# Moments in pairs on GpSimd, a seventh tile on VectorE, and a later adjacency load in the first stage of a graph kernel

## The chip, the cores and the metric

The kernel runs on one core of one Trainium2 chip. The metric is the device time of one execution in microseconds (us). The core has five engines with their own instruction streams: TensorE (PE, and PEld for its weight loads), VectorE (DVE), ScalarE (ACT), GpSimd (POOL) and SyncE (SP), which here only issues DMAs. They wait for each other by semaphores.

## The reference

```
def _layernorm(x):  m = mean(x); v = var(x); return (x - m) / sqrt(v + 1e-5)

h  = relu(_layernorm(x))                  # x: 8192 x 128
Wh = h @ W;  src = Wh @ a[:128];  dst = Wh @ a[128:]
e  = leaky_relu(src + dst.T, 0.2)         # 8192 x 8192
att = softmax(where(adj > 0, e, -9e15), axis=1)
h_prime = att @ Wh
...                                       # GRU cell with w_ih, w_hh, b_ih, b_hh on (h_prime, h)
x  = x + gru(h_prime, h)
h  = relu(_layernorm(x))
x  = x + adj @ (h @ W1.T + b1)
```

adj is an 8192 x 8192 float32 matrix of zeros and ones (256 MB).

## The kernel before, in words

The kernel has three stages. All run on five engines at once, each with its own loop. The order of work is written out by hand, and each instruction that another one needs raises a semaphore.

**First stage.** x lies in SBUF as 64 tiles H[:, t, :] of 128 rows x 128 columns. Eight DMAs bring eight tiles each (L264). VectorE makes the moments of a group q of eight tiles in `stats(q)`: bn_stats for each tile (L642), which leaves the mean and the sum of squared differences of the even and of the odd elements apart, bn_aggr, which joins them to mean and variance (L646), and the addition of EPS (L649). GpSimd raises the result to the power -0.5 in `deviation(q)` (L395). Then `normalised(q)` on VectorE: the product of mean and 1/deviation (L656), and `BY_DVE` = 6 of the eight tiles normalised (L659). ScalarE does the two others (L465). VectorE's order is stats(q+1), then normalised(q). TensorE transposes four tiles at a time (L999, k = 0 to 15, two for each q) into PSUM, ScalarE copies them with Relu (`column(k)`, L451), TensorE multiplies them with W and the two columns W @ a (`weighted(k)`, L987), and ScalarE copies the result to WG (`features(k)`, L455). TensorE may start the transposes only once VectorE has copied W @ a to wext (L672), which stands behind normalised(0).

SP's queue is in order too: for each k it waits for column(k) and stores it to memory (L275), for each odd k it stores eight tiles of H as rows (L278), and behind k = 7 and k = 15 it issues the loads of the first two pieces of the adjacency, X[0] and X[1], 2 MB each (L281). column(k) also waits until the store of column(k-4) has landed, whose buffer it reuses.

Then the tables. VectorE's instructions in order, the first of them right behind normalised(7):

```
ones_of(0, 0, 0, 0)                       # L692: X[0] -> bytes, waits for the load of X[0]
dve.wait_ge(p_ev, 16)                     # the last features()
... L699 to L714: largest and least of dst, signs, thresholds
table_product(0): L720 x2 (times TSCALE), then L728
```

ScalarE makes two tables of exponentials in between (L479, L480) and, behind them, calls one Sigmoid so that its table of functions is loaded (L483). table_product and table_low (VectorE, L728 and L733) and table_high (ScalarE, L490) make the tables TB for 16 groups; in row block 0 this is interleaved with the masks.

**Second stage.** 32 row blocks of 256 rows, four pieces c of each. VectorE makes ones of the adjacency (L692) and part of the sign masks (L743), ScalarE the others (L506), VectorE joins them (L751, L755), and TensorE multiplies masks and tables (L1014), 64 matmuls for each of 256 products. The GRU of earlier row blocks runs in between; its weights GW are made on GpSimd once (L416 to L420), right behind deviation(7) once their loads have landed, and its biases too (L401 to L412). **Third stage.** adj times the second features (L1104).

Of the kernel before, what the change touches and what calls it, by code (L numbers as in the profile page):

```python
# [1 line left out]

# [4 lines left out]
F = 128  # L7
P = 128
# [10 lines left out]
SLOPE = 0.2  # L19
# [5 lines left out]
EPS = 1e-5  # L25
# [7 lines left out]
TSCALE = 2048.0  # L33
# [9 lines left out]
GROUP = 5  # L43
COUNTED = (NS - 1) * CS
LATE = CS + 25
BY_DVE = 6

f32 = mybir.dt.float32
f16 = mybir.dt.float16
# [4 lines left out]
ALU = mybir.AluOpType  # L54
# [23 lines left out]
def binary_adjacency(nc, sem, q_out, redo, xb, adjb, w, wt, a, wiht, whht, b_ih, b_hh, w1t, b1, out):  # L78
    ctx = ExitStack()
    with ctx:  # L80
# [12 lines left out]
        JK = sb("JK", [P, 8 * TW])  # L93
# [55 lines left out]
        sdx = JK[:, 530:530 + NT]  # L149
        rsx = JK[:, 600:600 + NT]  # L150
        nmx = JK[:, 670:670 + NT]
        BG = X1[0].bitcast(bf16)
        bt, dt_ = BB[:, 0:NT], BB[:, NT:2 * NT]
        wtt = X1[0][:, 0:F]
# [49 lines left out]
        t_sc = k_w = sem("t_sc")  # L204
        d_hi = t_lo
        d_hh, d_hl = sem("d_hh"), sem("d_hl")
        g_sum = p_wa
        g_bb = p_ab
        g_pre = sem("g_pre")
# [50 lines left out]
        with nc.Block() as block:  # L260
            @block.sync
            def _(sp):
# [10 lines left out]
                for k in range(16):  # L273
                    sp.wait_ge(p_ht, k + 1)
                    sp.dma_start(ht_d[:, k * 512:(k + 1) * 512], hTq[k % 4]).then_inc(p_htout[k % 4], 16)  # L275
                    if k % 2:
                        q = k // 2
                        sp.dma_start(h_d[:, q * 8:(q + 1) * 8, :], H[:, q * 8:(q + 1) * 8, :]).then_inc(p_hout, 16)  # L278
                    if k in (7, 15):
                        b = k // 15  # L280
                        sp.dma_start(X[b][:, :], adjb[b, :, :]).then_inc(c_in[b], 16)  # L281
                    if k == 9:
                        sp.wait_ge(p_bias, 8)
                        for part in range(3):
                            sp.dma_start(b_d[part, :, :], bpart[part]).then_inc(b_in, 16)
# [90 lines left out]
            @block.gpsimd  # L376
            def _(pool):
                nc.gpsimd.memset(ident[:, :], 0.0).then_inc(p_id, 1)
                nc.gpsimd.memset(ones[:, :], 1.0)
                nc.gpsimd.memset(epst, EPS)  # L380
                nc.gpsimd.memset(half, -0.5)
                nc.gpsimd.memset(onesb[:, :], 1.0)
                nc.gpsimd.memset(nz[:, LATE - CS - 16:16, 2 * CS + 1:2 * CS + 2], 0.0)
                nc.gpsimd.memset(BI[:, :], 0.0).then_inc(p_one, 1)
                nc.gpsimd.memset(bhid, 0.0).then_inc(p_bias, 1)
                pool.wait_ge(p_id, 1)
                nc.gpsimd.affine_select(out=ident[:, :], in_=ident[:, :], compare_op=ALU.not_equal, fill=1.0,
                                        base=0, pattern=[[-1, P]], channel_multiplier=1).then_inc(p_id, 1)
                nc.gpsimd.memset(WG[:, :, F + 2:F + 3], 1.0).then_inc(p_one, 1)
                pool.wait_ge(p_one, 1)  # L390

                def deviation(q):
                    pool.wait_ge(p_sd, q + 1)
                    at = slice(q * 8, q * 8 + 8)
                    nc.gpsimd.tensor_tensor(rsx[:, at], sdx[:, at], half[:, 0:1].to_broadcast([P, 8]), ALU.pow).then_inc(  # L395
                        p_rs, 1)

                for q in range(4):
                    deviation(q)
                pool.wait_ge(p_wa, 1)  # L400
                nc.gpsimd.memset(X1[0], 0.0)  # L401
                pool.wait_ge(b_in, 80)
                nc.gpsimd.tensor_tensor(brow, brow, bhid, ALU.add).then_inc(p_bias, 1)
                pool.wait_ge(p_bias, 2)
                nc.gpsimd.tensor_scalar(brow[0:4, :], brow[0:4, :], WSCALE, None, ALU.mult).then_inc(p_bias, 1)
                src = [brow] + bres
                for k in range(3):
                    pool.wait_ge(p_bias, 2 * k + 3)
                    nc.gpsimd.tensor_copy(bpart[k], src[k]).then_inc(p_bias, 1)
                    if k < 2:  # L410
                        pool.wait_ge(p_bias, 2 * k + 4)
                        nc.gpsimd.tensor_tensor(bres[k], src[k], bpart[k], ALU.subtract).then_inc(p_bias, 1)  # L412
                for q in range(4, 8):
                    deviation(q)
                pool.wait_ge(wt_in, 64)
                nc.gpsimd.tensor_scalar(wraw, wraw, WSCALE, None, ALU.mult).then_inc(p_bias, 1)  # L416
                pool.wait_ge(p_bias, 9)
                nc.gpsimd.tensor_copy(GW[:, 0, :, :], wrawv).then_inc(p_bias, 1)
                pool.wait_ge(p_bias, 10)
                nc.gpsimd.tensor_tensor(GW[:, 1, :, :], wrawv, GW[:, 0, :, :], ALU.subtract).then_inc(p_bias, 1)  # L420
                pool.wait_ge(p_id, 2)
                nc.gpsimd.tensor_copy(identh[:, :], ident[:, :]).then_inc(p_bias, 1)

                def slot(g, u, k):
                    if in_range(g, 2):
                        q = g - 2
                        pool.wait_ge(d_mv, q + 1)
                        nc.gpsimd.tensor_tensor(ve, mv[:, :, 1:2].rearrange("p t k -> p (t k)"),  # L428
                                                epst[:, 0:1].to_broadcast([P, 2]), ALU.add).then_inc(d_ve, 1)
                        pool.wait_ge(d_ve, q + 1)  # L430
                        nc.gpsimd.tensor_tensor(rstd, ve, half, ALU.pow).then_inc(g_rs, 1)  # L431

                each_row_block(pool, slot)
                for g in range(NS, NS + 2):
                    slot(g, g % 2, g // 2)
# [200 lines left out]

            @block.vector
            def _(dve):
                def stats(q):
                    dve.wait_ge(p_x[q], 16)  # L640
                    for t in range(q * 8, q * 8 + 8):
                        ins = nc.vector.bn_stats(stx[:, t, :], H[:, t, :])  # L642
                    ins.then_inc(p_st, 1)
                    dve.wait_ge(p_st, q + 1)
                    for t in range(q * 8, q * 8 + 8):
                        ins = nc.vector.bn_aggr(mvx[:, t, :], stx[:, t, :])  # L646
                    ins.then_inc(p_mv, 1)
                    dve.wait_ge(p_mv, q + 1)
                    nc.vector.tensor_scalar(sdx[:, q * 8:(q + 1) * 8],  # L649
                                            mvx[:, q * 8:(q + 1) * 8, 1:2].rearrange("p t k -> p (t k)"), EPS, None,  # L650
                                            ALU.add).then_inc(p_sd, 1)
# [11 lines left out]
                    ins.then_inc(p_hd, 1)  # L663

                stats(0)
                for q in range(8):
                    if q < 7:
                        stats(q + 1)
                    normalised(q)
                    if q == 0:  # L670
                        dve.wait_ge(p_wa, 1)
                        nc.vector.tensor_copy(wext[:, 0:2], GP[:, 0:2]).then_inc(p_ab, 1)  # L672
# [35 lines left out]
                dve.wait_ge(p_dmt, 2)  # L708
                nc.vector.tensor_reduce(kt[:, 2:3], GP[:, 0:P], AX.X, ALU.max).then_inc(p_k, 1)
                dve.wait_ge(p_k, 1)  # L710
                nc.vector.tensor_scalar(kt[:, 0:1], kt[:, 2:3], -1.0, None, ALU.mult)
                nc.vector.tensor_scalar(kt[:, 1:2], kt[:, 2:3], -SLOPE, None, ALU.mult).then_inc(p_k, 1)
                nc.vector.tensor_scalar(sk, scol, kt[:, 2:3], 0.0, ALU.add, ALU.max).then_inc(p_sq, 1)
                nc.vector.tensor_copy(srow, GP[0:NT, P:2 * P]).then_inc(p_sq, 1)  # L714

                def table_product(i):
                    if i == 0:
                        for n, table in enumerate((bt, dt_)):
                            dve.wait_ge(p_exp, n + 1)
                            nc.vector.tensor_scalar(table, table, TSCALE, None, ALU.mult).then_inc(t_sc, 1)  # L720
                        dve.wait_ge(p_one, 2)
                        for b in range(2):
                            dve.wait_ge(p_htout[b], 64)
                        dve.wait_ge(t_sc, 2)
                    wait(dve, t_lo, i - 1)
                    j, m = i // 2 * 8, i % 2
                    by = (bt, dt_)[m][:, j:j + 8].rearrange("p (j o) -> p j o", o=1).to_broadcast([P, 8, TW])
                    nc.vector.tensor_tensor(PB[i % 2], WG[:, j:j + 8, 2:F + 3], by, ALU.mult).then_inc(t_p, 1)  # L728
# [28 lines left out]
                def gate_step(qh, u, n, q):  # L757
# [9 lines left out]
                        nc.vector.tensor_tensor(tmp[:, :, :], rz[:, :, 0:F], GP3[:, :, 3 * F:4 * F], ALU.mult).then_inc(  # L767
                            d_rh, 1)
                    if halving:
                        dve.wait_ge(d_hh, qh + 1)  # L770
                        nc.vector.tensor_tensor(HH[:, 1, :], HT[u], HH[:, 0, :], ALU.subtract).then_inc(d_hl, 1)
                    if gating:
                        dve.wait_ge(d_rh, q + 1)
# [164 lines left out]
                                                   ALU.add).then_inc(k_df, 1)  # L938

                def judge():  # L940
                    dve.wait_ge(k_w, 3)
                    nc.vector.tensor_reduce(bad[:, 3:4], GP[:, 0:1], AX.X, ALU.max).then_inc(k_v, 1)
                    nc.vector.tensor_reduce(bad[:, 4:5], GP[:, P:2 * P], AX.X, ALU.max).then_inc(k_v, 1)
                    nc.vector.tensor_scalar(bad[:, 7:8], bad[:, 0:1], GMOST * GSCALE, None, ALU.is_le).then_inc(k_v, 1)
# [873 lines left out]
```

## Time and profile before

| what | value |
|---|---|
| time, median of 3 runs | 1553.67 us (1552.84 to 1554.71) |
| the profiled execution | 1554.47 us, span of its instructions 1552.9 us |
| mean granted TensorE clock | 0.984 |
| busy share of the span | PE 96%, DVE 89%, ACT 88%, POOL 9% |
| moved by DMA | 502.93 MB, mean 324 GB/s |

The span is from the first to the last instruction. Busy shares are averages over three stages with different limits; the first stage ends at some 45 us, the first product of the second starts at 61 us. The granted clock is 1.00 at 2.4 GHz.

### The profile page before, as it was taken

Reading aid. Unit: us, or ns where it says so; the run is one execution under the profiler, and the core shown is the slowest. Engines: PE = TensorE matmul, PEld = TensorE weight load, DVE = VectorE, ACT = ScalarE, POOL = GpSimd, SP = SyncE. Lnnn points to the kernel's source line nnn. Section 1 sums busy time; section 2 is a strip of 40 time slices with the busy share of each in tenths; the row PEclk is TensorE's granted clock in tenths of the full one; section 3 lists DMA queues with packets and bytes.
Section 4 is the critical chain, followed back from the end, with each engine's and each line's share of the span. In section 5 each row is a group of like instructions: output and inputs, shape, how many; then the busy total and the mean of one; then the engine's idle time right before and its main releaser. Section 6 shows DMA issues by size and latency. Waiting matters only on the chain.

```text
span 1552.9 us, 35381 instructions
## 1 busy us (share of the span) xinstructions
PE 1485.6 (96%) x13262; PEld 1304.4 (84%) x13262; DVE 1386.0 (89%) x2256; ACT 1369.6 (88%) x1972; POOL 136.2 (9%) x98
## 2 busy tenths in 40 slices
PE   5477999999999999999999999999999999999998
PEld 5356888888888888888888888888888888888887
DVE  8997999999999999999999999997579877766684
ACT  5779999999999999999999999996185998777785
POOL 5000011001100010001000100010000000000000
PEclk9778999999999999999999999999999999999999
DMA  8858999999999999999999999996386999888860
GB/s 314 298 204 332 365 350 360 352 366 353 355 357 370 352 349 353 374 351 357 359 365 345 362 362 355 349 360 265 122 354 238 408 361 352 308 304 310 321 228 16
DMA packets 96380, 502.93 MB, mean 324 GB/s; under 512 B 9599, under 2 KB 38985, under 8 KB 75337
## 3 DMA queue, kind: packets, MB, share of 16 engines
q1 hardware_dynamic: 78328, 444.54, 76.1%
q10 hardware_dynamic: 18000, 57.74, 9.8%
q8 instruction: 28, 0.46, 0.1%
q14 instruction: 24, 0.19, 0.0%
HBM read 418.32 MB, written 83.92 MB: 323 GB/s over the span
## 4 chain that ended last, share of the span: by engine, by line
PE 92%; DVE 5%; ACT 1%; issue 1%; DMA 0%; POOL 0%; DVEq 0%; ACTq 0%
PE ACC L1014 57%; PE ACC L1104 29%; PE GP L1040 2%; PE GP L1043 2%; PE GQ L1061 1%; ACT M L506 1%; DVE M L659 1%; DVE JK L642 1%; DVE TB L733 1%; DVE AE L728 1%; DVE JK L728 1%; PE TG L1027 0%; PE TG L1050 0%; DVE JK L646 0%; DVE M L751 0%
## 5 line engine op out<-in xcount | busy, mean ns | idle before, releaser
L1014 PE MATMUL ACC<-TB,M 128*128 128x258 f16 x8192 | 927.2, 275 | 41.8 <-DVE M L751 30.7
L1014 PEld LDWEIGHTS ACC<-TB,M 128*128 128x128 fp8e4 x8192 | 804.5, 98 | 150.7 <-issue 43.2
L506 ACT ACTIVATE M<-SB,dsteep 128x256 fp8e4<-128x256 f32 x1273 | 526.2, 538 | 0.0
L516 ACT ACTIVATE JK<-X 128x3328 uint8<-128x3328 uint32 x124 | 373.2, 3010 | 0.0
L692 DVE TENSOR_SCALAR Y<-X 128x4096 fp8e4<-128x4096 f32 x128 | 291.9, 2280 | 5.9 <-DMA X<-in_adjb_dram 5.5
L605 ACT ACTIVATE TB<-TB 128x8192 uint8<-128x8192 fp8e4 x32 | 225.0, 7030 | 76.5 <-DVE TB L890 71.7
L1104 PE MATMUL ACC<-WG,X 128*128 128x256 f16 x2048 | 225.5, 273 | 0.0
L1104 PE MATMUL ACC<-WG,TB 128*128 128x256 f16 x2048 | 225.4, 273 | 0.0
L1104 PEld LDWEIGHTS ACC<-WG,X 128*128 128x128 fp8e4 x2048 | 200.4, 98 | 23.2
L1104 PEld LDWEIGHTS ACC<-WG,TB 128*128 128x128 fp8e4 x2048 | 200.4, 98 | 23.1
L743 DVE TENSOR_SCALAR M<-SB,nd 128x256 fp8e4<-128x256 f32 x775 | 213.7, 345 | 0.0
L751 DVE TENSOR_TENSOR M<-M,Y 128x1024 uint32<-128x1024 uint32 x128 | 155.7, 1217 | 7.7 <-ACT M L506 7.0
L755 DVE TENSOR_TENSOR M<-Y,M 128x1024 uint32<-128x1024 uint32 x128 | 156.8, 1225 | 4.4
L428 POOL TENSOR_TENSOR few<-mv,few 128x2 f32<-128x2 f32 x32 | 65.0, 2032 | 963.1 <-DVE mv L834 963.1
L890 DVE TENSOR_TENSOR TB<-X 128x8192 fp8e4<-128x8192 fp8e4 x16 | 138.9, 8689 | 4.0 <-ACT TB L605 2.7
L890 DVE TENSOR_TENSOR TB<-TB 128x8192 fp8e4<-128x8192 fp8e4 x16 | 138.9, 8681 | 1.5 <-ACT TB L605 1.5
L623 ACT ACTIVATE JK<-M 128x3840 uint8<-128x3840 uint32 (+2 forms) x29 | 98.5, 3395 | 0.9 <-DMA M<-in_adjb_dram 0.9
L906 DVE SCALAR_TENSOR_TENSOR hp<-ACC,R 128x256 f32<-128x256 f32 x32 | 13.5, 423 | 95.6 <-PE ACC L1104 93.4
L431 POOL TENSOR_TENSOR few<-few 128x2 f32<-128x2 f32 x32 | 48.3, 1510 | 2.5
L526 ACT ACTIVATE AE<-ACC 128x516 f32<-128x516 f32 x64 | 40.1, 627 | 5.8 <-PE ACC L1014 5.8
L1040 PE MATMUL GP<-GW,hpT 128*128 128x384 f16 x192 | 41.7, 326 | 0.0
L1043 PE MATMUL GP<-GW,HH 128*128 128x384 f16 x192 | 41.7, 326 | 0.0
(145 smaller groups left out, 786.9 us busy)
## 6 DMA issues: line engine op xcount, KB each, us to landing
X<-in_adjb_dram SPq DMA_DIRECT2D x128, 2048.0 KB, 9.8
mask_bytes<-Y SPq DMA_DIRECT2D x128, 512.0 KB, 5.1
M<-in_adjb_dram ACTq DMA_DIRECT2D x24, 1920.0 KB, 9.8
X<-mask_bytes SPq DMA_DIRECT2D x16, 2048.0 KB, 9.5
TB<-mask_bytes SPq DMA_DIRECT2D x16, 2048.0 KB, 9.1
M<-in_adjb_dram ACTq DMA_DIRECT2D x4, 2048.0 KB, 11.9
M<-in_xb_dram SPq DMA_DIRECT2D x8, 512.0 KB, 8.3
h_rows<-M SPq DMA_DIRECT2D x8, 512.0 KB, 3.9
```

Of the source, the lines that this page charges most:

```text
L506: ins = nc.scalar.activation(rows(mask1(c), jj), SB[u][:, :], ACT.Sigmoid, scale=STEEP, bias=dsteep[:, j:j + 1], saturate=False)
L516: nc.scalar.activation(junk[:, 0:SEEN], X[c % 2][:, 0:SEEN].bitcast(u32), ACT.Sign, accum_out=nz[:, bass.ds(k, 1), at:at + 1].rearrange("p ...
L605: nc.scalar.activation(junk8, halves[t % 2], ACT.Copy, accum_out=cy[:, t:t + 1]).then_inc(q_sum, 1)
L623: nc.scalar.activation(junk[:, 0:cols], Z[n % 2][:, 0:cols].bitcast(u32), ACT.Sign, accum_out=nz[:, k:k + 1, at:at + 1].rearrange("p k c - ...
L692: nc.vector.tensor_scalar(Y[c % 2][:, :].bitcast(f8), X[c % 2][:, :], 1.0, MARK, ALU.is_equal, ALU.mult, saturate=False).then_inc(c_y, 1)
L743: ins = nc.vector.tensor_scalar(rows(mask1(c), jj), SB[u][:, :], nd[:, j:j + 1], None, ALU.is_ge, saturate=False)
L751: nc.vector.tensor_tensor(mask1(c), mask1(c), Y[c % 2][:, :], ALU.bitwise_and).then_inc(c_m1, 1)
L755: nc.vector.tensor_tensor(mask2(c), Y[c % 2][:, :], mask1(c), ALU.bitwise_xor).then_inc(c_m2, 1)
L890: nc.vector.tensor_tensor(halves[b % 2], YB[b][:, 0:N], YB[b][:, N:2 * N], ALU.add, saturate=False).then_inc(q_half, 1)
L1014: ins = nc.tensor.matmul(A[t][m][:, 0:2 * TW], rows((mask1, mask2)[m](c), jj)[:, t * P:(t + 1) * P], TB[:, c * JC + jj, m, 0:2 * TW], star ...
L1040: nc.tensor.matmul(bank[:, 0:3 * F], left, GW[:, part, 0, :], start=False, stop=False, skip_group_check=True)
L1104: ins = nc.tensor.matmul(PH2[b][:, d * 2 * F:(d + 1) * 2 * F], YB[b][:, j * RW + d * P:j * RW + (d + 1) * P], GS[:, j, :], start=(d == 0 a ...
```

## The change

- Groups 0 and 1 keep `stats` as it was. For groups 2 to 7 VectorE only does bn_stats (`halves_stats`), two groups in a row: 2 and 3 behind normalised(0), 4 and 5 behind normalised(1), 6 and 7 behind normalised(3). GpSimd joins the halves for a pair of groups (16 tiles) in `pair_moments`: seven small instructions on 128 x 16 elements and the power.
- `BY_DVE` is 7: VectorE normalises seven of eight tiles, ScalarE one.
- X[0] is loaded behind k = 11 instead of k = 7.
- GpSimd starts on the weights of the gates only when VectorE has done all its tiles (p_hd at 16).
- The factor TSCALE goes into the bias of the two exponentials, and L720 falls away.

```diff
-BY_DVE = 6
+BY_DVE = 7
...
-                    if k in (7, 15):
+                    if k in (11, 15):
...
+                def pair_moments(p):
+                    at = slice(p * 16, p * 16 + 16)
+                    mean_e, part_e, mean_o, part_o = [stx[:, at, i:i + 1].rearrange("p t k -> p (t k)") for i in (1, 2, 4, 5)]
+                    mean = mvx[:, at, 0:1].rearrange("p t k -> p (t k)")
+                    pool.wait_ge(p_st, 2 * p + 2)
+                    nc.gpsimd.tensor_tensor(px[0], mean_e, mean_o, ALU.add).then_inc(p_ag, 1)
+                    nc.gpsimd.tensor_tensor(px[1], part_e, part_o, ALU.add).then_inc(p_ag, 1)
+                    pool.wait_ge(p_ag, p * 6 - 5)
+                    nc.gpsimd.tensor_scalar(mean, px[0], 0.5, None, ALU.mult).then_inc(p_ag, 1)
+                    pool.wait_ge(p_ag, p * 6 - 4)
+                    nc.gpsimd.tensor_scalar(px[1], px[1], 1.0 / F, EPS, ALU.mult, ALU.add).then_inc(p_ag, 1)
+                    pool.wait_ge(p_ag, p * 6 - 3)
+                    nc.gpsimd.tensor_tensor(px[0], mean_e, mean, ALU.subtract).then_inc(p_ag, 1)
+                    pool.wait_ge(p_ag, p * 6 - 1)
+                    nc.gpsimd.tensor_tensor(px[0], px[0], px[0], ALU.mult).then_inc(p_ag, 1)
+                    pool.wait_ge(p_ag, p * 6)
+                    nc.gpsimd.tensor_tensor(sdx[:, at], px[1], px[0], ALU.add).then_inc(p_sd, 1)
+                    pool.wait_ge(p_sd, p + 2)
+                    nc.gpsimd.tensor_tensor(rsx[:, at], sdx[:, at], half[:, 0:1].to_broadcast([P, 16]), ALU.pow).then_inc(
+                        p_rs, 2)
+
-                for q in range(4):
+                for q in range(2):
                     deviation(q)
+                pair_moments(1)
...
-                for q in range(4, 8):
-                    deviation(q)
+                for p in range(2, 4):
+                    pair_moments(p)
+                pool.wait_ge(p_hd, 16)
                 pool.wait_ge(wt_in, 64)
                 nc.gpsimd.tensor_scalar(wraw, wraw, WSCALE, None, ALU.mult).then_inc(p_bias, 1)
...
-                def stats(q):
+                def halves_stats(q):
                     dve.wait_ge(p_x[q], 16)
                     for t in range(q * 8, q * 8 + 8):
                         ins = nc.vector.bn_stats(stx[:, t, :], H[:, t, :])
                     ins.then_inc(p_st, 1)
+
+                def stats(q):
+                    halves_stats(q)
                     dve.wait_ge(p_st, q + 1)
...
                 stats(0)
+                stats(1)
                 for q in range(8):
-                    if q < 7:
-                        stats(q + 1)
                     normalised(q)
+                    if q in (0, 1, 3):
+                        for ahead in range(q + q % 2 + 2, q + q % 2 + 4):
+                            halves_stats(ahead)
                     if q == 0:
                         dve.wait_ge(p_wa, 1)
                         nc.vector.tensor_copy(wext[:, 0:2], GP[:, 0:2]).then_inc(p_ab, 1)
...
-                nc.vector.tensor_scalar(kt[:, 0:1], kt[:, 2:3], -1.0, None, ALU.mult)
-                nc.vector.tensor_scalar(kt[:, 1:2], kt[:, 2:3], -SLOPE, None, ALU.mult).then_inc(p_k, 1)
+                nc.vector.tensor_scalar(kt[:, 0:1], kt[:, 2:3], -1.0, math.log(TSCALE), ALU.mult, ALU.add)
+                nc.vector.tensor_scalar(kt[:, 1:2], kt[:, 2:3], -SLOPE, math.log(TSCALE), ALU.mult, ALU.add).then_inc(p_k, 1)
...
                     if i == 0:
-                        for n, table in enumerate((bt, dt_)):
-                            dve.wait_ge(p_exp, n + 1)
-                            nc.vector.tensor_scalar(table, table, TSCALE, None, ALU.mult).then_inc(t_sc, 1)
                         dve.wait_ge(p_one, 2)
                         for b in range(2):
                             dve.wait_ge(p_htout[b], 64)
-                        dve.wait_ge(t_sc, 2)
+                    if i < 2:
+                        dve.wait_ge(p_exp, i + 1)
```

The rest of the diff counts semaphores anew (p_ag is another name of d_hh, k_w of t_sc).

## Rows read from the trace of the kernel before

**Rows 1.** The page's chain that ended last, by engine.
```profile
PE 92%; DVE 5%; ACT 1%; issue 1%; DMA 0%; POOL 0%; DVEq 0%; ACTq 0%
```

**Rows 2.** Chain in order of time: start us, us, what.
```profile
5.16 1.65 DVE JK L642 x8
...
22.37 1.88 DVE M L659 x6
...
24.85 1.56 DVE JK L642 x8
...
27.11 0.17 DVE JK L649
...
27.35 1.54 DVE M L659 x6
...
35.44 1.75 POOL JK L395
...
37.92 4.08 DVE M L659 x6
...
42.05 0.66 PE GQ L999 x4
...
45.22 0.26 DVE bad L699
...
142.16 7.04 PE ACC L1014 x64
```

**Rows 3.** Timeline of PE and SPq, k = 7 to 9: start us, us, instruction.
```profile
25.18 0.60 PE L999 MATMUL GQ<-ident,M 128*128 128x128 f32 x4
...
27.78 0.43 SPq L281 DMA_DIRECT2D X<-in_adjb_dram  x1
...
28.43 0.66 PE L999 MATMUL TG<-ident,M 128*128 128x128 f32 x4 [1.75 <-DVE M L659]
...
29.81 0.60 PE L999 MATMUL GQ<-ident,M 128*128 128x128 f32 x4
```

**Rows 4.** Line L281, issue to landing of X[0] and X[1].
```profile
DMA to landing us min/median/max: 8.7/9.2/9.7
```

**Rows 5.** GpSimd, L659 and L692: timeline rows, and lines (ns min/median/max, first and last start).
```profile
20.03 0.31 POOL L401 MEMSET R<- 128x256 f32 x1
...
21.79 0.42 POOL L412 TENSOR_TENSOR TB<-TB 5x128 f32<-5x128 f32 x1
...
23.12 0.28 POOL L409 CAST TB<-TB 5x128 bf16<-5x128 f32 x1
...
40.27 1.64 POOL L420 TENSOR_TENSOR GW<-R,GW 128x768 f16<-128x768 f32 x1
...
41.91 2.38 DVE L692 TENSOR_SCALAR Y<-X 128x4096 fp8e4<-128x4096 f32 x1
...
L395 POOL TENSOR_TENSOR JK<-JK,few x8: 1650/1738/1742, 7.8 to 35.4; 128x8 f32<-128x8 f32 x8
...
L428 POOL TENSOR_TENSOR few<-mv,few x32: 196/2151/3288, 170.0 to 1120.1; 128x2 f32<-128x2 f32 x32
...
L659 DVE TENSOR_SCALAR M<-M,JK x48: 334/340/1809, 10.1 to 40.2; 128x128 f32<-128x128 f32 x48
```

**Rows 6.** Timeline of the tables' start.
```profile
47.81 1.28 ACT L483 ACT_TABLE_LOAD   x1
...
48.00 1.23 DVE L728 TENSOR_TENSOR AE<-WG,BB 128x1032 f32<-128x1032 f32 x1
```

**Rows 7.** Stretch (PE, PEld, DVE, ACT, POOL busy, PEclk, DMA share, GB/s); timeline of PE.
```profile
48.00:62.00 14.00, 0.52 (x3) 0.42 (x4) 13.35 (x11) 11.91 (x22) 0.00 (x0) 0.50 0.86 325
...
76.11 9.99 PE L1014 MATMUL ACC<-TB,M 128*128 128x258 f16 x64 [5.83 <-DVE M L751]
...
105.22 9.11 PE L1014 MATMUL ACC<-TB,M 128*128 128x258 f16 x64 [5.00 <-DVE M L751]
...
125.87 16.06 PE L1014 MATMUL ACC<-TB,M 128*128 128x258 f16 x128 [11.11 <-issue]
```

More of the change, by code:

```diff
@@ L1 @@
 from contextlib import ExitStack
+import math
 import concourse.bass as bass
@@ L151, in binary_adjacency @@
         nmx = JK[:, 670:670 + NT]
+        px = [JK[:, 740 + 20 * i:740 + 20 * i + 16] for i in range(2)]
         BG = X1[0].bitcast(bf16)
@@ L206, in binary_adjacency @@
         d_hh, d_hl = sem("d_hh"), sem("d_hl")
+        p_ag = d_hh
         g_sum = p_wa
@@ L769, in gate_step @@
                     if halving:
-                        dve.wait_ge(d_hh, qh + 1)
+                        dve.wait_ge(d_hh, 18 + qh + 1)
                         nc.vector.tensor_tensor(HH[:, 1, :], HT[u], HH[:, 0, :], ALU.subtract).then_inc(d_hl, 1)
@@ L940, in judge @@
                 def judge():
-                    dve.wait_ge(k_w, 3)
+                    dve.wait_ge(k_w, 1)
                     nc.vector.tensor_reduce(bad[:, 3:4], GP[:, 0:1], AX.X, ALU.max).then_inc(k_v, 1)
```

## The prediction

> **What bounds the kernel now.** I read the page's chain first. Nine tenths of it is TensorE in the two big products [rows 1]; the change touches none of these instructions, so it can only move the moment at which they start. So next the chain of work in order of time for the first 145 us, to see what sets that moment. From 5.16 us, when the first eighth of x has landed, to 42 us every piece but one is VectorE: the moments and the normalising of x [rows 2]. A period is 4.04 us for eight tiles (27.35 + 1.54 less 24.85): 1.58 of L642 (bn_stats), then 0.68 of L646 (bn_aggr) up to 27.11, 0.17 of L649 (add EPS) and 0.07 of L656 up to 27.35, and 1.54 of six L659. The last period is broken: the power on GpSimd is waited for (35.44), and the last six L659 take 4.08 instead of 1.54. Then a tail of 3.2 us on TensorE and ScalarE: the last transposes at 42.05, x@W, its copy, and at 45.22 L699, the first VectorE step of the tables. From there to the first matmuls of the main loop nothing is free: tables and masks follow one another on VectorE and ScalarE, so a shift of L699 is a shift of the end, one for one.
>
> The instruction ahead of L699 on VectorE is L692 (ones_of), which turns the first adjacency piece X[0] into bytes. It needs that piece landed. Before, it was issued at 27.78 [rows 3] and took at most 9.7 us [rows 4], so it lay ready at 37.5, and L692 at 41.91 [rows 5] waited for nothing. This is the slack that the change spends.
>
> **The change, part by part.** I number the transposes T(0) to T(15), four tiles each; column(k) is their copy on ScalarE (L451).
>
> VectorE loses bn_aggr and the add in six of eight periods (0.85 us each, 5.1 in all) and gains a seventh L659 in eight (1.54/6 = 0.257 each, 2.1 in all). It also changes order: two groups of bn_stats stand together, then two groups are normalised. Two full stats take 2 x 2.43, so the first L656 is at 5.16 + 4.86 = 10.02, as now. One normalised group is 0.08 + 7 x 0.257 = 1.88, a bn_stats group behind another 1.56. T(8) can begin when four tiles of group 4 are normalised: 10.02, plus groups 0 to 3 (7.52), plus six bn_stats groups (9.36), plus the wext copy (0.07), plus the diagonal of q = 3 (24.85 less 24.25 in [rows 2], 0.60), plus 0.08 + 4 x 0.257 + 0.1 to TensorE: 28.8 us. (Now T(8) is at 28.43 [rows 3]: up to there almost nothing is gained, since six of the eight stats are done by then and the seventh tiles are paid. Only from there on is VectorE faster, 1.88 against 4.04 a group.)
>
> GpSimd gets seven small instructions and a power of 16 columns for each of three pairs. None of this shape is in the trace. Lower bound for a small one 0.20 (L428's shortest, 2 columns), upper 0.42 (L412, 128 columns) [rows 5]; 16 columns are near the lower, so 0.23 and 0.08 between them: 2.1 us. The power takes 1.65 to 1.74 for 8 columns; I take 1.85 for 16. A pair is 4 us. Pair 1 runs from 15.1 to about 19.2, and group 2 wants it at 20.1: hidden, under the bn_stats of groups 4 and 5. The bias steps follow behind it on GpSimd (now 20.0 to 23.4), so pair 2 ends near 27 with group 4 wanting it at 28.5; pair 3, whose moments are there near 28, ends at 32 with group 6 wanting it at 32.5. Each is hidden by 0.5 to 1 us. Without that cover a pair's lateness falls on VectorE one for one.
>
> What the small instructions cost VectorE: where three bias steps of 128 columns overlapped six L659, these took 1.88 instead of 1.54 [rows 2], 0.11 for each. Some 17 small ones of the pairs and seven of the bias steps can meet L659 ahead of T(8): at 0.11 each 2.6 us; nothing if all meet bn_stats, beside which no row shows a delay. By columns (0.34 us for 384) it is 0.2 for the pairs and 0.8 for the bias steps. I take 1.0, and 0 to 2.6 as bounds: T(8) at 29.8, from 28.8 to 31.4.
>
> Two rows disagree on this. The last L659 took 1.81 us beside L420's 1.64 [rows 5], held till that ended; but beside the powers of 1.74 us the six L659 keep their 1.54. The Trainium skill (SBUF — State Buffer, "Who interferes with whom") says that a GpSimd instruction keeps the port pair that it shares with VectorE for its whole length and that the other blocks fully. The row of L420 agrees with it, the rows of the power don't; by it the time would be that of rival (b), 1560.2, by the rows of the power the sum below.
>
> wext now comes behind two bn_stats groups, so T(0) starts at 15.2 instead of 11.9. TensorE needs 1.38 us from one T to the next (28.43 to 29.81) and VectorE takes 3.44 on average for the eight tiles of two, so this is made up by T(8). From T(8) on TensorE is the slower one: T(11) is at 29.8 + 3 x 1.38 = 33.9, T(15) at 39.5 (VectorE would be done at 37). That alone would bring the tail's end, L699, to 39.5 + 3.2 = 42.7, 2.5 us earlier than now.
>
> ScalarE loses one of two L465 a period; it was not the bound. The column stores no longer stand behind X[0] for k = 8 to 11: that takes away the one wait of column(12). The weights of the gates wait for p_hd 16, thus for the end of L659. Now they run from the power's end, 37.2, to L420's, 41.9: 4.7 us of GpSimd work, which moves to between 37 and 42, when VectorE has nothing to do but wait (next paragraph). That takes away the 2.5 us of the long last L659; behind it on GpSimd only identh is queued, and its next readers are far.
>
> Now the moved load. It is issued behind column(11) instead of column(7), past four column stores, two row stores and the bias stores on SP's queue. Before, T(7) was at 25.18 and the issue at 27.78, 2.6 later [rows 3], with the same two stores just ahead of it. Then it is issued at 33.9 + 2.6 = 36.5. Landing takes 8.7 to 9.7 [rows 4]; I take 9.2: **45.7**. L692 takes 2.3, so L699 stands at 48.0 against 45.22: **+2.8 us**. Bounds: T(8) at 28.8 and landing in 8.7 give 46.5, +1.3; 31.4 and 9.7 give 50.1, +4.9. Everything gained ahead of it is idle time of VectorE before L692. X[1] and the last stores move in the same queue and land near 54; they are wanted near 60.
>
> The two scalings by TSCALE fall away: the first L728 is at 48.00 and could follow 0.6 us earlier. But ScalarE's table load lies at 47.81 for 1.28 us [rows 6], and the first conversion can't start before 49.1 whatever L728 does, against 48.00 + 1.23 now. So at most 0.15 is gained: -0.1.
>
> TensorE's clock: it stands at 0.50 from 48 to 62 us (the 1.2 GHz level) [rows 7], and the bursts of block 0 go through it: 64 matmuls take 9.99, then 9.11 us where at the full 2.4 GHz level they take 7.04; 128 take 16.06 at 125.87. Two of these are on the chain [rows 7]. With other starting times each may come out from 2.1 us less to 0.9 more; the two last ones are already near the short end of what is seen, so +0.3, bounds -1 and +1.5.
>
> Sum: +2.8 - 0.1 + 0.3 = **+3.0 us**. The profiled execution took 1554.47 (span 1552.9), so it would take 1557.5; it lies 0.8 above the median shown, 1553.67, and the time forecast is **1556.7 us**. What a measurement can tell from no change is 0.2%, 3.1 us, so this is just inside "same".
>
> **Rivals.**
> (a) *The load costs nothing or little.* For it: without any contention and with a landing of 8.7 us the shift is +1.3, and the clock can take it back. Against: the bounds must all fall one way. Time: 1553.5 to 1555. Chance 0.18.
> (b) *GpSimd holds or keeps VectorE waiting* (the other side: slower). Each small instruction holds L659 for its whole length: 0.23 x 17 for the pairs and 0.35 x 7 for the bias steps make 6.4 us ahead of T(8) instead of 1.0, less what falls on bn_stats, say 4.5: X[0] is issued 3.5 us later still, 1560.2 us. It decides from a T(8) later than 30. The same follows if a pair takes 6 us instead of 4, since then groups 2, 4 and 6 each wait. For it: L420 above, and L428, which takes 2.15 as a rule behind an L692. Against: the powers. Chance 0.17. The rule of the Trainium skill named above (SBUF — State Buffer, "Who interferes with whom") is this rival.
> (c) *TensorE or VectorE sets the end and not the load.* Then L699 would stand at 42.7 and the time be 1551. X[0] would have to land by 40.4, 3.9 us after an issue at 36.5, where the shortest landing of [rows 4] is 8.7; and from the lower bound of T(8) that landing still gives +1.3. So over 0.2% faster also needs both bursts far nearer to 7.04. Chance 0.05.
> My forecast holds 0.60: +1.5 to +4.5, 1555.2 to 1558.2, with a little more below the 3.1 us than above.
>
> **The numbers.** Faster by over 0.2%: 0.05 (c). Slower: 0.17 (b) and 0.28 of the forecast, 0.45. Same: the other 0.32 of it and (a), 0.50. The range leaves out (c) and the ends of (a) and (b): 1553.4 to 1559.8.
>
> **What would show it.** Right: L692 first starts near 45.7 released by the DMA of X, with VectorE idle ahead of it for 8 us; T(8) near 29.8, T(11) near 34, transposes 1.38 apart; L699 near 48; the GpSimd weights inside the idle time; the main loop as before. Wrong: L692 released by VectorE or before 43; a wait of VectorE for the power in groups 2, 4 or 6 of over 1 us; L659 groups of 7 over 2.5 us; or TensorE bursts at 105 and 125 us that differ by more than 1 us from those of before.

## The result, and the profile after

The changed kernel takes 1559.31 us (median of 7, 1557.24 to 1560.12) against 1553.02 of the kernel before in the same comparison (7, 1552.71 to 1554.71). The ratio is 1.0033, 95% interval 1.0024 to 1.0042, so it is slower by 3.7 to 6.5 us. The forecast was 1556.7, with 1553.4 to 1559.8 as its range: the direction and the range held, the size was too small (the sum was +3.0, the ratio says +5.1, and the forecast lies 2.6 us under the median), and "within 0.2%" had been given a little more chance (0.50) than the "slower" (0.45) that came.

The page of the changed kernel's profile first: the chain by engine, and the group that the prediction named. (The lines have moved: L642 is now L669, L656 L686, L659 L689, L692 L724, L699 L731, L728 L758, L999 L1029, L1014 L1044, the load of X[0] L285.)

```profile
PE 92%; DVE 4%; ACT 2%; DMA 1%; issue 1%; SPq 0%; DVEq 0%; ACTq 0%
...
L724 DVE TENSOR_SCALAR Y<-X 128x4096 fp8e4<-128x4096 f32 x128 | 291.8, 2280 | 17.3 <-DMA X<-in_adjb_dram 17.1
```

Against [rows 1] DMA has come into the chain with 1%. VectorE stands idle ahead of L724 for 17.3 us in the whole span, 17.1 of them for loads of X. The chain in order of time (start us, us, what) shows where:

```profile
28.45 1.05 DVE M L689 x4
...
29.54 1.12 PE TG L1029 x4
30.66 1.73 PE ACC L1017 x8
32.39 0.73 PE GQ L1029 x4
...
37.46 9.63 DMA X<-in_adjb_dram
...
47.24 2.29 DVE Y L724
49.53 0.17 DVE bad L731
...
109.36 9.83 PE ACC L1044 x64
...
130.73 16.44 PE ACC L1044 x128
```

To be read against [rows 2, 3]: the piece that was not there before is the load, 9.63 us. L731 comes at 49.5 instead of 45.2, 4.3 us late, and everything behind it keeps that; the two bursts on the chain add 9.83 less 9.11 and 16.44 less 16.06 [rows 7], 1.1 more. Together that is the 5.4 us by which the two spans differ (1558.3 less 1552.9).

TensorE and the granted clock (columns as in [rows 7]) around the end of its idle time:

```profile
26.00:29.50 3.50, 1.26 (x11) 1.03 (x9) 3.46 (x19) 2.12 (x5) 3.34 (x6) 0.99 1.00 391
29.50:31.00 1.50, 1.46 (x7) 1.46 (x8) 1.50 (x7) 0.30 (x1) 1.20 (x4) 0.50 0.29 107
31.00:33.00 2.00, 2.00 (x12) 2.00 (x12) 1.15 (x5) 0.86 (x2) 2.00 (x1) 0.53 0.36 135
33.00:40.00 7.00, 7.00 (x65) 6.94 (x64) 3.84 (x16) 6.04 (x14) 2.97 (x3) 1.00 0.79 284
```

TensorE had nothing to do for 2.3 us before T(8), and from 29.5 to nearly 33 it worked at the 1.2 GHz level. The last view is VectorE's and GpSimd's timeline:

```profile
15.00 1.88 DVE L689 TENSOR_SCALAR M<-M,JK 128x128 f32<-128x128 f32 x7
...
16.93 2.93 POOL L420 TENSOR_TENSOR JK<-JK,few 128x16 f32<-128x16 f32 x1
...
19.97 2.55 DVE L689 TENSOR_SCALAR M<-M,JK 128x128 f32<-128x128 f32 x7
...
22.52 2.13 DVE L689 TENSOR_SCALAR M<-M,JK 128x128 f32<-128x128 f32 x7
...
33.28 0.17 DVE L686 SCALAR_TENSOR_TENSOR JK<-JK 128x8 f32<-128x8 f32 x1 [1.13 <-POOL JK L420]
...
35.23 1.88 DVE L689 TENSOR_SCALAR M<-M,JK 128x128 f32<-128x128 f32 x7
...
37.20 2.14 POOL L443 TENSOR_SCALAR R<-R 128x768 f32<-128x768 f32 x1 [3.96 <-DVE M L689]
...
47.24 2.29 DVE L724 TENSOR_SCALAR Y<-X 128x4096 fp8e4<-128x4096 f32 x1 [10.12 <-DMA X<-in_adjb_dram]
```

VectorE is through with x at 37.1, 4.9 us sooner than before, and then stands idle for 10.12 us.

### The profile page after: what moved, and what is told of

Same layout as the page of the kernel before. It is cut to its first block, busy times and chain, and to the rows that moved or that the text cites. A ratio compares the mean times of both kernels' runs of the same rounds, so it can differ in the third digit from the quotient of the medians.

```text
span 1558.3 us, 35373 instructions
## 1 busy us (share of the span) xinstructions
PE 1485.7 (95%) x13262; PEld 1305.6 (84%) x13262; DVE 1380.0 (89%) x2208; ACT 1366.0 (88%) x1964; POOL 139.7 (9%) x116
## 4 chain that ended last, share of the span: by engine, by line
PE 92%; DVE 4%; ACT 2%; DMA 1%; issue 1%; SPq 0%; DVEq 0%; ACTq 0%
PE ACC L1044 57%; PE ACC L1134 29%; PE GP L1070 2%; PE GP L1073 2%; PE GQ L1091 1%; ACT M L533 1%; DVE JK L669 1%; DMA X<-in_adjb_dram 1%; DVE TB L763 1%; DVE M L689 1%; DVE JK L758 1%; DVE AE L758 1%; PE TG L1057 0%; PE TG L1080 0%; ACT TB L517 0%
## 5 line engine op out<-in xcount | busy, mean ns | idle before, releaser
L1044 PE MATMUL ACC<-TB,M 128*128 128x258 f16 x8192 | 927.1, 275 | 42.8 <-DVE M L781 31.6
L1044 PEld LDWEIGHTS ACC<-TB,M 128*128 128x128 fp8e4 x8192 | 804.5, 98 | 151.7 <-issue 44.2
L724 DVE TENSOR_SCALAR Y<-X 128x4096 fp8e4<-128x4096 f32 x128 | 291.8, 2280 | 17.3 <-DMA X<-in_adjb_dram 17.1
## 6 DMA issues: line engine op xcount, KB each, us to landing
X<-in_adjb_dram SPq DMA_DIRECT2D x128, 2048.0 KB, 10.1
```

The costliest lines, as they stand in the source:

```text
L724: nc.vector.tensor_scalar(Y[c % 2][:, :].bitcast(f8), X[c % 2][:, :], 1.0, MARK, ALU.is_equal, ALU.mult, saturate=False).then_inc(c_y, 1)
L1044: ins = nc.tensor.matmul(A[t][m][:, 0:2 * TW], rows((mask1, mask2)[m](c), jj)[:, t * P:(t + 1) * P], TB[:, c * JC + jj, m, 0:2 * TW], star ...
```

## The experiments

Each ratio is against the kernel before, measured with it on the same chip (10 or 11 runs of each kernel, 8 of warm, and about 30 of the kernel before); a per mille is 1.55 us. "Table step" is the start of the first VectorE step of the tables (L731, or L699 in the kernel before; the number moves by a line or two with the edit). Each kernel has one profile. In these the first bn_stats starts between 4.8 and 5.7 us, when the first eighth of x has landed, and all that follows in this stage moves with it, so a difference of under 1 us between two table steps is not a reading by itself.

**b11: the late load alone, in the kernel before.**

```diff
-                    if k in (7, 15):
+                    if k in (11, 15):
```

> The kernel before with one part of the change alone: X[0] is loaded behind k = 11 instead of k = 7. My theory: T(11) at 33.9, the load issued at 36.5, landed at 45.2 to 46.2, first table step at 47.5 to 48.5 instead of 45.2; time 1555.3 to 1556.5. Rival (the load is not what counts): the table step stays at 45.2 or comes sooner, since column(12) no longer waits for a store behind X[0]; time 1552 to 1553.5.

Ratio 1.0018 (1.0008 to 1.0028), 2.8 us slower (1.2 to 4.4). Its chain:

```profile
36.22 9.52 DMA X<-in_adjb_dram
...
45.88 2.29 DVE Y L692
48.18 0.17 DVE bad L699
```

As expected, this one line delays the table step from 45.2 to 48.2. Nothing of GpSimd's new work is in this kernel. The median, 1557.44, lies above the 1556.5 expected, but the kernel before took 1554.76 in this comparison and not the 1553.67 from which I had counted.

**x7: the changed kernel with the load put back.**

```diff
-                    if k in (11, 15):
+                    if k in (7, 15):
```

> The changed kernel with one part undone: X[0] is loaded behind k = 7 again. My theory (the late load holds up VectorE's ones_of and with it the tables): the load is issued near 28 and lands near 37.6, when VectorE is done with its tiles at 37.1; ones_of then meets the gate weights on GpSimd, and column(12) waits again for a store behind X[0], so the first table step, at 49.5 in the changed kernel, is at 44.5 to 46; time 1554 to 1556. Rival (the small GpSimd instructions and the new order cost the time, not the load): the table step stays at 48 or later and the time at 1558 or more.

Ratio 1.0002 (0.9992 to 1.0012): with the load back the slowdown is gone, and so is any gain. Timeline:

```profile
37.87 4.25 POOL L443 TENSOR_SCALAR R<-R 128x768 f32<-128x768 f32 x1 [3.96 <-DVE M L689]
...
39.14 2.29 DVE L724 TENSOR_SCALAR Y<-X 128x4096 fp8e4<-128x4096 f32 x1 [1.36 <-DMA X<-in_adjb_dram]
...
39.72 0.60 ACT L478 ACTIVATE AE<-TG 128x512 f32<-128x512 f32 x1 [2.88 <-DMA h_columns<-AE]
...
45.90 0.26 DVE L731 TENSOR_REDUCE bad<-WG 128x1 f32<-128x64 f32 x1 [4.46 <-ACT WG L482]
```

VectorE is free at 41.4 and waits 4.46 us for the features. What holds them is column(12), which waits 2.88 us for the store of column(8), issued behind the load: the wait of 1.5 us before, grown, since the columns now come faster. The theory's two numbers (44.5 to 46, 1554 to 1556) hold; the rival's 1558 does not.

**x3: the load earlier still.**

```diff
-                    if k in (11, 15):
+                    if k in (3, 15):
```

> The changed kernel with X[0] loaded behind k = 3. My theory: it lands near 32, before VectorE is free at 37.1, and no column waits behind it; T(15) stays near 40.6 and the first table step comes at 43.7 to 44.5; time 1552 to 1554. Rival (GpSimd costs the time): table step at 48 or later, 1558 or more. A second rival, that the gate weights of 37.2 to 42 hold ones_of off until 42: table step at 44.3 all the same, since the features end at 43.8.

Ratio 1.0005 (0.9996 to 1.0015). I was wrong here: the load does lie ready at 37.2, but the stores behind it are late. The store of column(4) takes 9.28 us, ScalarE stands idle for 4.43 us ahead of column(8), which waits for it, and for 0.59 ahead of column(10). The last row is TensorE's stretch behind this wait:

```profile
33.86 0.60 ACT L478 ACTIVATE AE<-TG 128x512 f32<-128x512 f32 x1 [4.43 <-DMA h_columns<-AE]
...
47.08 0.27 DVE L731 TENSOR_REDUCE bad<-WG 128x1 f32<-128x64 f32 x1 [7.60 <-ACT WG L482]
...
33.00:40.00 7.00, 5.49 (x34) 5.49 (x35) 6.03 (x17) 4.25 (x8) 3.05 (x2) 0.76 1.04 410
```

A load of 2 MB ahead of stores on which the columns wait four steps later takes back what its early landing gives. It doesn't cost as much as the late one (1.0033). And a part of the late table step is the clock: TensorE was idle for 2.80 us, then the granted clock was at its low level from 35 to 38, and T(11) came 2.52 us behind T(10) instead of 1.38.

**order: the load stays late, the tables no longer queue behind it.**

```diff
-                ones_of(0, 0, 0, 0)
                 dve.wait_ge(p_ev, 16)
...
+                            if first and c == 0:
+                                ones_of(0, 0, 0, 0)
                             if c < CS - 1:
```

> The changed kernel with the load of X[0] left where it is, behind k = 11, but VectorE's first ones_of moved behind the first four table products and their low parts, so that the table steps no longer queue behind it. My theory (what costs is that queue, not the load itself): the first table step comes at 43.7 to 44.5, when the last features are there, instead of 49.5; ones_of then costs its 2.3 us on the chain, of which 0.5 is idle time now; in all 3.5 to 4 us less than the changed kernel, 1555 to 1556. Rival (a late load also holds up the rest, or GpSimd's work does): less than 2 us gained.

Ratio 1.0006 (0.9997 to 1.0015), 2.7 per mille or 4.2 us under the changed kernel's 1.0033; 3.5 to 4 were expected.

```profile
44.04 0.27 DVE L730 TENSOR_REDUCE bad<-WG 128x1 f32<-128x64 f32 x1 [6.71 <-ACT WG L482]
```

The table step is at 44.0 with the load where it was. So it is VectorE's queue behind L724 that costs, not the load as such. The chain of this kernel shows what comes next: ScalarE's masks wait until 52.6 for the last store of H's rows (10.06 us from its issue).

**warm: eight matmuls of no use ahead of T(8).**

```diff
                 for k in range(16):
+                    if k == 8:
+                        for _ in range(8):
+                            nc.tensor.matmul(GP[:, 512:512 + P], ones[:, :], ident[:, :], start=True, stop=True)
                     pe.wait_ge(p_hd, k + 1)
```

> The changed kernel with eight matmuls of no use (128 x 128, float32, into a free half of GP) on TensorE ahead of its wait for T(8), where it stood idle from 27.3 to 29.5 and then worked at a granted clock of 0.50 until 33. If that low clock is what put T(9) 2.64 behind T(8) instead of 1.38, the clock stays at 1.00, T(9) follows by 1.4, X[0] is issued 1.2 sooner and the first table step is at 48.1 to 48.5 instead of 49.5; time 1558. Rival (T(9) waited for ScalarE or VectorE): T(9) is still 2.6 behind and nothing moves.

One stretch (columns as above), TensorE's timeline and the chain:

```profile
29.50:31.00 1.50, 1.13 (x11) 0.94 (x10) 1.50 (x8) 0.24 (x2) 1.12 (x6) 1.00 0.56 223
```
```profile
30.13 0.66 PE L1032 MATMUL TG<-ident,M 128*128 128x128 f32 x4 [0.37 <-DVE M L689]
...
31.51 0.60 PE L1032 MATMUL GQ<-ident,M 128*128 128x128 f32 x4
```
```profile
36.54 11.67 DMA X<-in_adjb_dram
...
48.36 2.29 DVE Y L724
```

The first half is right: the clock stays at 1.00, T(9) follows T(8) by 1.38, and the load is issued at 36.54 instead of 37.46, though x landed 0.56 later here. The second half is not: it lands in 11.67 us instead of 9.63, at 48.2, so the table step is at 50.7. What is issued behind the load doesn't tell the two kernels apart: the next store follows 0.72 us after it (0.81 in the changed kernel), the load of X[1] 5.29 (5.39). Why it took 2 us more is not shown. Ratio 1.0034 (1.0023 to 1.0045): no time gained. The time lies 3.4 us above the span here, 1.6 to 1.8 in the others; the median span, 1556.9, is 3.9 above that of the kernel before in the same comparison (1553.0).

**gw: the gate weights alone moved, in the kernel before.**

```diff
+                pool.wait_ge(p_hd, 16)
                 pool.wait_ge(wt_in, 64)
```

> The kernel before with the gate weights alone moved: GpSimd starts on them when VectorE has done its last tile. The six L659 of the last group take 1.6 instead of 4.08, VectorE is done near 39.5, and TensorE's own pace with the wait of column(12) puts T(15) at 41.0 to 41.5: first table step 44.2 to 44.7 instead of 45.2; time 0.5 to 1 us less. Rival (ones_of meets the weights and is blocked by them): ones_of ends at 44 or later and the table step stays at 45 or comes later.

Ratio 0.9998 (0.9989 to 1.0008). The last group of L659 takes 1.63 and VectorE is done at 39.0, but the table step stays:

```profile
29.88 8.75 DMA h_columns<-AE
...
38.72 0.60 ACT L452 ACTIVATE AE<-TG 128x512 f32<-128x512 f32 x1 [1.82 <-PE GQ L1000]
...
45.28 0.26 DVE L700 TENSOR_REDUCE bad<-WG 128x1 f32<-128x64 f32 x1 [4.02 <-ACT WG L456]
```

The theory's 44.2 to 44.7 is missed. The rival has the right table step for a wrong reason: ones_of, from 38.97, held the weights and not they it. In the chain this column(12) hangs on the store of column(8), which took 8.75 us (the timeline names TensorE for the wait; its T(12) was done at 37.3, 1.4 us before). Two limits lay within a microsecond of each other: the 4 us of L659 beside the weights, and the store behind the load. Removing one shows the other.

**fold: TSCALE in the exponentials alone.**

```diff
-                nc.vector.tensor_scalar(kt[:, 0:1], kt[:, 2:3], -1.0, None, ALU.mult)
+                nc.vector.tensor_scalar(kt[:, 0:1], kt[:, 2:3], -1.0, math.log(TSCALE), ALU.mult, ALU.add)
...
-                            nc.vector.tensor_scalar(table, table, TSCALE, None, ALU.mult).then_inc(t_sc, 1)
```

> The kernel before with TSCALE folded into the exponentials alone. The first table product starts 0.6 sooner, but ScalarE's table load ends where it did, so the first conversion starts at most 0.15 sooner; no difference in the time that can be measured. Rival (the scalings are on the path): conversion and time 0.5 less.

Ratio 1.0002 (0.9992 to 1.0011). The table step is at 46.37 here, in a part that the edit doesn't touch: x landed 0.3 later, and column(12) waited for a store of 9.65 us. From it to ScalarE's table load it is 2.58 us, as before (47.81 less 45.22, [rows 2, 6]), and the load is on the chain, where the scalings were in its shadow:

```profile
48.95 1.28 ACT L485
...
50.44 0.97 ACT TB L492
```

**xfirst: the load ahead of all stores.**

```diff
+                sp.dma_start(X[0][:, :], adjb[0, :, :]).then_inc(c_in[0], 16)
                 sp.wait_ge(p_x[7], 16)
...
-                    if k in (11, 15):
-                        b = k // 15
+                    if k == 15:
+                        b = 1
```

> The changed kernel with X[0] loaded ahead of all column stores, right behind the loads of x and of the biases. It should land near 22, the stores of columns 0 to 3 behind it. TensorE has 2 us of idle time ahead of T(8) that can take the delay of columns 4 to 7, so T(15) stays at 40.5 to 41.5 and the first table step comes at 43.7 to 44.7; ones_of starts at 37.2 and keeps the gate weights waiting, not the other way round. Time 0.5 to 1.5 us under the kernel before. If the stores are held up as behind k = 3 (9.3 us to landing), a column waits for 3 us or more and the table step is at 46 to 47.

Ratio **0.9986 (0.9977 to 0.9995)**, 2.2 us faster than the kernel before (0.8 to 3.6): the version that beats both. The load line, TensorE's timeline, the chain, and GpSimd's timeline:

```profile
DMA to landing us min/median/max: 14.9/14.9/14.9
```
```profile
29.55 0.66 PE L1030 MATMUL TG<-ident,M 128*128 128x128 f32 x4 [2.40 <-DVE M L690]
...
30.94 0.60 PE L1030 MATMUL GQ<-ident,M 128*128 128x128 f32 x4
```
```profile
42.24 0.26 DVE bad L732
42.51 1.49 DVE nn L733
```
```profile
37.21 4.11 POOL L444 TENSOR_SCALAR R<-R 128x768 f32<-128x768 f32 x1 [3.96 <-DVE M L690]
...
42.29 1.64 POOL L448 TENSOR_TENSOR GW<-R,GW 128x768 f16<-128x768 f32 x1
```

Issued at 7.0 it lands at 21.9, behind x and before any column needs a buffer again. The table step is at 42.2, 1.5 sooner than the least that I said. The clock didn't fall in this execution, and that is the 1.5: from T(8) to the table step it is 12.69 us here and 14.27 in order, where it fell. Then the second step is held for 1.37 us by L448, the end of the gate weights, which ones_of had held up.

**best and bestwarm: without the wait of the gate weights, and with the matmuls too.**

```diff
-                pool.wait_ge(p_hd, 16)
                 pool.wait_ge(wt_in, 64)
```

> As xfirst (X[0] loaded ahead of the column stores), and the gate weights no longer wait for the end of VectorE's tiles: they start behind the last pair of moments, near 33.3. In xfirst they ran from 37.2 to 43.9 and held the second table step (nn) for 1.37 us. Now they lie beside the last two groups of L690, which get 2.5 to 3 us longer, but TensorE is behind VectorE there: VectorE done near 40, T(15) at 39.5 to 40.5. First table step at 42.3 to 43.5 and nothing held behind it; 0.3 to 1.4 us less than xfirst, near 1551.5. Rival (VectorE becomes the bound again): T(15) after 40.5, no gain over xfirst.

> As best, with the eight matmuls of no use ahead of T(8). In some executions of the changed order TensorE's granted clock fell to 0.5 behind its idle time at 27 to 29.5 and T(9) came 1.2 late, in others it stayed. If these matmuls keep it up, the median is 0.3 to 1 us under that of best; rival: no difference, or more, since they are work.

best: ratio 0.9994 (0.9985 to 1.0003), no better than xfirst; the gain that I expected didn't come. The rival of that run is right:

```profile
34.77 3.26 DVE M L689 x3
38.08 0.66 PE GQ L1029 x4
```

Three of VectorE's tiles take 3.26 beside the weights, and TensorE now waits for them for T(13). The clock fell in the profile of best and not in that of bestwarm, and the table step is at 44.0 and 44.2 all the same: VectorE is the bound in both. bestwarm: 1.0003 (0.9994 to 1.0012). Its median span, 1551.7, is like best's 1551.3, but the time lies 3.6 us above the span instead of 1.6. In warm it was 3.4, in all other kernels 1.6 to 1.8.

**bfirst and bfirstgw: the kernel before with the early load, and with the gate weights moved as well.** The edits are those of xfirst and gw.

> The kernel before with X[0] loaded ahead of the column stores and nothing else. Column(12) no longer waits for a store, but VectorE's last six L659 still take 4.08 beside the gate weights and end at 42.0, so T(15) and the first table step stay (45.2); same time as before within 0.5 us. Rival (the wait of column(12) is the bound by itself): 1 us less.

> The kernel before with both: X[0] ahead of the column stores, and the gate weights after VectorE's last tile. With neither wait left VectorE is done near 39.1 and T(15) comes at 40.5 to 41; first table step at 43.7 to 44.2, but the gate weights, held off by ones_of, run till 46 and hold the second step for 1 to 1.5 us, so 0.2 to 1 us less than before. If the moments on GpSimd are worth anything by themselves, xfirst (1552.4) stays 1 us or more below this one.

bfirst: 0.9999 (0.9990 to 1.0009); bfirstgw: 1.0000 (0.9991 to 1.0009). Rows of their chains, in this order:

```profile
37.56 4.08 DVE M L660 x6
...
44.87 0.26 DVE bad L700
```
```profile
44.22 0.27 DVE bad L701
44.48 1.38 DVE nn L702
```

In bfirst the 4.08 us of the last six tiles are still there. In bfirstgw both limits are gone and VectorE's 4.04 a group is what is left: table step at 44.2, and nearly the same hold of the next step as in xfirst, 1.26 us. The hold takes what the sooner table step gives, and the 0.2 to 1 us that I expected can't be seen. xfirst has the table step at 42.2; so the moments on GpSimd, with the seventh tile, are worth some 2 us (0.9986 against 1.0000), but only with the load out of the way. These two ratios come from two comparisons and their intervals touch, so the 2 us are a rough figure, and what the moments and the seventh tile do each by itself was not tried.

## Why the forecast was right, and where it was too small

- *The load queues the tables.* Shown from three sides: put alone into the kernel before it costs 2.8 us (b11), taken back it returns all (x7), and taken out of VectorE's way it returns nearly as much without being moved (order). L724 started when the load landed, with VectorE idle ahead of it, as said, for 10.1 us where I had said 8. In b11 the load is issued 1.2 us sooner than in the changed kernel (36.22), where TensorE's clock stayed at 1.00.
- *T(8) at 29.8*: 29.5. The small instructions cost L689 next to nothing: the seven of pair 1 lie inside a group of 1.88. What lengthened groups 2 and 3 (2.55 and 2.13) is mostly the bias steps, which run from 20.1 to 23.3. Together 0.9 us, where I had put 1.0. Rival (b), that GpSimd holds VectorE, is refuted for instructions of 16 columns. Its 1560.2 us is nearer to the measured time than my 1556.7, but by its own sign, a T(8) later than 30, it is not what happened.
- *A pair takes 4 us*: 4.9, since the power of 16 columns takes 2.93 and not 1.85. Group 6 waited 1.13 us for it; TensorE was behind, so it cost nothing. Two of my signs of being wrong thus came up, this wait of over 1 us and a group of over 2.5 (2.55), without either setting the time.
- *T(11) = T(8) + 3 x 1.38 = 33.9*: **this is the term that was mis-sized.** T(11) was at 35.2. I had counted TensorE's clock in the table stage but not here, although my own sum left TensorE idle for 2 us ahead of T(8). The clock fell, T(9) came 2.64 behind T(8) and T(10) 1.67 behind that: the three steps took 5.64 instead of 4.14, 1.5 us more. That the low clock made T(9) late is shown by the profiles together: where it fell (after, order, best) T(9) is 2.64 to 2.65 behind T(8), where it stayed (x7, x3, xfirst, warm, bestwarm) 1.38 to 1.39, with no wait of TensorE in between.
- *Issue 2.6 behind T(11), landing 9.2 later*: 2.3 and 9.6. In warm the same load took 11.7, and X[1] 13.9 in the changed kernel, so my upper bound of 9.7, the longer of two landings before, was no bound.
- *Table step 48.0*: 49.5, +4.3 instead of +2.8.
- *The two scalings -0.1*: the shift is 4.3 at the table step and 4.2 at the first conversion (53.43 against 49.27). fold confirms that there is nothing in it.
- *Bursts +0.3*: +1.1, inside the bounds given. Of the 2.4 us between my +3.0 and the +5.4 of the spans, 1.5 are the table step, 0.8 the bursts and 0.1 the scalings.
- *Gate weights in VectorE's idle time*: as said, 37.2 to 42.2, and worth nothing as long as the load is late.

Rival (a) needed all bounds to fall one way; TensorE's steps and the landing went the other way. Rival (c) needed the load off the path, and it was on it. What stays open: the runs of the changed kernel lie in two groups (two at 1557.2 and 1557.3, five from 1559.3 to 1560.1), which would fit a clock that falls in some executions and not in others. The clock granted over the whole span fits too: 0.984 and 0.983 in the two, 0.980 to 0.982 in the five. The profile is of one of the five. If this is so, the two executions that kept the clock lie within 1 us of the forecast, and the other five are what it missed. But only one execution has a profile, so this is argued and not shown.

## What to carry to other kernels

When a transfer is moved later to unclog a queue, look for the first instruction that needs it and for what stands behind that instruction on its engine: a transfer of 9 us that was ready 4 us early turns into a wait of 10 when everything ahead of it becomes faster too. A place where nobody waits for either side (here behind the loads of x, ratio 0.9986) beat the later ones tried (behind k = 3, 7 and 11: 1.0005, 1.0002, 1.0033). And where two limits end within a microsecond of each other, test the edits together: here the gate weights alone, the early load alone, the two together, the weights with GpSimd's moments (x7), and the load with them (best) gave nothing that is clear of the noise; all three gave 2.2 us.

## What was unexpected of the hardware

- TensorE's granted clock can fall behind a short idle time. Behind 2.29, 2.31, 2.39 and 2.80 us (after, order, best, x3) it was 0.50 for some 3.5 us of dense work; behind 2.40 and 2.78 (xfirst, x7) it stayed at 1.00, and behind 1.42 and 1.32 (x7, x3) too. With matmuls laid into the idle time it stayed in both kernels that have them (warm, bestwarm). As it also stayed in some without, one profile of each doesn't show that the matmuls kept it.
- The landing time of one 2 MB load is no constant: X[0] behind k = 11 took 9.5 us (b11), 9.6 (changed kernel) and 11.7 (warm), the last two with the next store and the load of X[1] at the same distances behind it, and 14.9 behind the loads of x (xfirst). The cause of the 2 us is open.
- The power on GpSimd takes 1.56 us for 2 columns, 1.74 for 8 and 2.93 for 16.
- Which of VectorE and GpSimd yields is not only a matter of who is first. L443 takes 2.14 alone and 4.1 to 4.25 beside a ones_of, which keeps its 2.29; L448 (TENSOR_TENSOR, 768 columns) holds a small VectorE step for 1.37. The Trainium skill (SBUF — State Buffer, "Who interferes with whom") says that where a VectorE instruction in a two-port mode meets GpSimd, whoever issues first gets the shared pair for the whole instruction and the other blocks (the profile doesn't show the mode). xfirst agrees: ones_of starts at 37.03, L444 at 37.21 and takes 4.11. x7 doesn't: L443 starts at 37.87, ones_of 1.27 us behind it at 39.14, and it is still L443 that is held. The powers and the small instructions, beside which L689 keeps its pace, don't agree either, and the same tiles are held beside the gate weights (best), so the form of L689 can't be the difference.
- Eight matmuls more left the span of best about as it was (1551.7 against 1551.3), yet the time outside the span was 3.4 and 3.6 us in the two kernels that had them and 1.6 to 1.8 in all others. The cause is open.
